# Four small-head attentions: ScalarE's exponentials of a sequence in one run, and a copy moved from ScalarE to VectorE

## The reference, cut to what matters

```python
def heads(x):                       # (8, 128, 128) -> (8, 16, 128, 8)
    return x.reshape(B, S, 16, 8).transpose(0, 2, 1, 3)
qh, kh, vh = heads(q @ wq + bq), heads(k @ wk + bk), heads(v @ wv + bv)
scores = einsum('bhqd,bhkd->bhqk', qh, kh) / sqrt(8)
scores = where(mask, -inf, scores)  # in the first and the last layer only
out = einsum('bhqk,bhkd->bhqd', softmax(scores), vh)
x = x + merge(out) @ wo + bo        # the first layer has an MLP in place of wo
```

## Time and profile before

| | |
|---|---|
| median of 3 runs | 1392.16 us (1392.0 to 1392.6) |
| the profiled execution | 1387.83 us, span 1386.0 us |
| mean granted TensorE clock | 0.896 |
| TensorE matmul busy | 1144.6 us (83%) |
| VectorE busy | 790.0 us (57%) |
| ScalarE busy | 654.6 us (47%) |
| exponentials of the four attentions (line 873) | 128, 69.0 us, mean 598 ns |

### The profile page before, as it was taken

One profiled execution on the slowest core, in us unless ns is written; L12 is line 12 of the kernel. 1 busy time (PEld: TensorE's weight loads), 2 busy tenths in 40 slices (PEclk: granted clock), 3 DMA queues, 4 the chain that ended last, 5 costly groups with the idle time before them and its releaser, 6 DMA issues. The chain is left out here.

```text
span 1386.0 us, 25064 instructions
## 1 busy us (share of the span) xinstructions
PE 1144.6 (83%) x9532; PEld 734.7 (53%) x9532; DVE 790.0 (57%) x1974; ACT 654.6 (47%) x1370; POOL 325.8 (24%) x321
## 2 busy tenths in 40 slices
PE   6998895559798987759877973979889988898998
PEld 4565453337465653327635742847434444465776
DVE  3565446567565458887787878456362565452111
ACT  2564333441253225586687672534666442334332
POOL 1333200013301003754546440140000034300000
PEclk9999998566799997887997996899899998899999
DMA  7000000200000000000000000061095700000000
GB/s 298 1 2 1 1 2 1 90 4 1 0 3 1 0 1 0 0 1 2 1 1 2 2 1 1 2 258 84 17 200 125 153 1 2 1 2 1 1 1 16
DMA packets 15206, 44.39 MB, mean 32 GB/s; under 512 B 1872, under 2 KB 4976, under 8 KB 14448
## 3 DMA queue, kind: packets, MB, share of 16 engines
q1 hardware_dynamic: 15088, 42.80, 10.6%
HBM read 42.01 MB, written 0.79 MB: 31 GB/s over the span
## 5 line engine op out<-in xcount | busy, mean ns | idle before, releaser
L873 ACT ACTIVATE L_xattn_pT<-banks 128x512 f32<-128x512 f32 x128 | 69.0, 598 | 107.2 <-PE banks L757 107.2
L243 POOL TENSOR_TENSOR norm_rstd<-norm_var,norm_power 128x4 f32<-128x4 f32 x24 | 24.6, 1025 | 365.6 <-DVE norm_var L236 365.6
L927 DVE TENSOR_REDUCE L_xattn_top<-banks 128x4 f32<-128x512 f32 x128 | 79.5, 685 | 43.4 <-PE banks L728 43.4
L1511 DVE TENSOR_TENSOR L_ffn_a<-L_ffn_a,L_ffn_share 128x512 f32<-128x512 f32 x64 | 39.9, 687 | 60.2 <-DMA L_ffn_share<-L_ffn_shares 60.0
L1425 PE MATMUL banks<-L_ffn_a,region_a 128*128 128x512 f32 x136 | 67.5, 601 | 5.1 <-DVE L_ffn_a L1511 5.1
L1744 ACT ACTIVATE L_ffn_aT<-banks,L_ffn_shift 128x512 f32<-128x512 f32 x64 | 43.3, 687 | 58.9 <-PE banks L1696 57.3
L1416 PE MATMUL banks<-hT,region_a 128*128 128x512 f32 x136 | 68.9, 612 | 0.0
L1757 DVE SCALAR_TENSOR_TENSOR x<-banks,L_ffn_combine,x 128x128 f32<-128x128 f32 x64 | 18.0, 345 | 88.7 <-PE banks L1707 88.7
L1707 PEld LDWEIGHTS banks<-region_b,L_ffn_aT 128*128 128x128 f32 x512 | 59.4, 192 | 6.7 <-issue 6.7
L492 ACT ACTIVATE L_attn_p<-banks,L_attn_shift 128x129 f32<-128x129 f32 x128 | 45.4, 369 | 35.6 <-DVE L_attn_shift L542 35.6
L1580 PE MATMUL banks<-hT,region_a 128*128 128x512 f32 x128 | 59.4, 608 | 1.3 <-PEq L78 1.3
(11 more groups left out here) (532 smaller groups left out, 2932.1 us busy)
## 6 DMA issues: line engine op xcount, KB each, us to landing
L_ffn_share<-L_ffn_shares SPq DMA_DIRECT2D x32, 512.0 KB, 10.1
region_b<-in_L_ffn SPq DMA_DIRECT2D x1, 6216.0 KB, 29.5
region_a<-in_L_ffn SPq DMA_DIRECT2D x1, 4416.0 KB, 14.1
region_b<-in_L_attn SPq DMA_DIRECT2D x1, 3150.5 KB, 11.6
region_a<-in_L_ffn SPq DMA_DIRECT2D x1, 3080.5 KB, 21.6
region_b<-in_L_attn SPq DMA_DIRECT2D x1, 1633.5 KB, 10.3
region_b<-in_L_xattn SPq DMA_DIRECT2D x1, 835.0 KB, 10.9
w_tables<-in_tables SPq DMA_DIRECT2D x1, 832.0 KB, 13.6
```

The costliest lines, as they stand in the source:

```text
L873: nc.scalar.activation(pT[:, n % 2, 4 * i:4 * i + 4, :], rows_of(flip[i][:], 4), ACT.Exp, scale=scale).then_inc(exped, 1)
L927: nc.vector.tensor_reduce(top[:, 32 * i:32 * i + 32:HD], rows_of(score[i][:], 4), X, ALU.max).then_inc(topped, 1)
L1511: nc.vector.tensor_tensor(a[:, k % AHEAD, :], a[:, k % AHEAD, :], share[:, batch % RING, j, :], ALU.mult).then_inc(weighed, 1)
```

## The change

ScalarE runs the four exponentials of a sequence one after the other and then keep_out; keep_raw leaves it. VectorE does keep_raw(k-2) between find_top(k) and keep_top(k), as a tensor copy. Nothing else is changed: tiles, banks, semaphores and their counts stay.

```diff
@@ ScalarE
-            def keep_raw(n):
-                act.wait_ge(mixed, n + 1)
-                nc.scalar.activation(raw[:], rows_of(mix[:, 0:2 * T], 2), ACT.Copy).then_inc(raw_kept, 1)
-
...
             for k in range(1, LAST):
                 if 0 <= k - 1 < B:
-                    weigh(k - 1, (0, 1))
-                if 0 <= k - 2 < B:
-                    keep_raw(k - 2)
+                    weigh(k - 1, range(G))
                 if 0 <= k - 3 < B:
                     keep_out(k - 3)
-                if 0 <= k - 1 < B:
-                    weigh(k - 1, (2, 3))
                 if carries and k == B + 2:
                     ahead.keep(act, 0, score[2])
@@ VectorE
+            def keep_raw(n):
+                dve.wait_ge(mixed, n + 1)
+                nc.vector.tensor_copy(raw[:], rows_of(mix[:, 0:2 * T], 2)).then_inc(raw_kept, 1)
...
                 if k < B:
                     find_top(k)
+                if 0 <= k - 2 < B:
+                    keep_raw(k - 2)
+                if k < B:
                     keep_top(k)
                 if 0 <= k - 4 < B and out_weight is not None:
                     add(k - 4)
```

## The result

The changed kernel takes 1401.14 us (median of 10 runs, 1397.85 to 1410.73) against 1392.38 us (10 runs, 1386.08 to 1393.8). The ratio on record is 1.0081, 95% interval 1.0057 to 1.0105: slower by 0.8%, where 0.43% was forecast. It is not the quotient of the two medians, which is 1.0063 (+8.8 us); the interval goes with the ratio. The median lies 0.5 us above the range. The profiled execution took 1398.14 us, span 1396.3 us at a mean clock of 0.894; the one of before took 1387.83 us, span 1386.0 us.

The account below looks back on a forecast made before the run. TensorE was taken as the bound. The attentions' terms, +1.72 (first), +1.94 (last) and +1.18 for each unmasked one, made +6.0 us; on the median of 1392.16 that gave 1398.2 us (+0.43%), range 1395.6 to 1400.6.

Parts of the forecast that it names:

- Part 1: Scores of sequences 4 to 7 wait for the later keep_out: +2.20 us a masked attention, +1.44 an unmasked one.
- Part 2: Raw copy on VectorE, 0.40 us long, delays keep_top in step 2: +0.02 us an attention.
- Part 3: Attention ends: flipped scores -0.05 us; last mixing -0.45 us in the first attention, -0.23 in the other three.
- The attentions' sum: All four attentions: first +1.72, last +1.94, the two unmasked +1.18 each, together +6.0 us.
- The early exponentials win: Exponentials and keep_out finish before scores are wanted, only gains left: 1390.2 us; chance 0.03 beyond 0.2%, 0.03 within.
- The delay is partly given back: Scores to E shortens by 0.2 us in each of 16 sequences: 1395.0 us; chance 0.08.
- VectorE becomes the bound: Raw copy of 0.54 us makes keep_top and the norm's work late: +1.3 us, 1399.5 us; chance 0.07.
- The clock falls: Added TensorE idle in the attentions halves its clock for one sequence in each: +12 us, 1410 us; chance 0.03.

Follow-up runs that it names:

- ends alone: Against the kernel before: four exponentials in a row and VectorE's raw copy only in steps 8 and later; 1396.50 us, ratio 1.0050.
- delays: Kernel before, steps untouched, plus useless copies at each attention's end (ScalarE in the first, VectorE in the others), some 6.6 us in all; 1399.67 us, ratio 1.0072.
- keep_out between the pairs: Changed kernel with keep_out put back between the second and third exponential, raw copy still on VectorE; 1393.87 us, ratio 1.0038.
- keep_out alone behind: Kernel before with only keep_out moved behind the last exponential, raw copy still on ScalarE between the pairs; 1402.63 us, ratio 1.0085.
- late wait: Changed kernel with score banks written in the order 0, 2, 3, 1 and the wait for keep_out only before bank 1; 1396.47 us, ratio 1.0060.
- first two attentions: Kernel before with the change only in the attentions of the first two layers, ahead of the delta rule; 1397.61 us, ratio 1.0059.
- last attention: Kernel before with the change only in the last layer's attention, behind which one stage follows; 1393.92 us, ratio 1.0021.
- third attention: Kernel before with the change only in the third layer's attention, which stands behind the delta rule; 1391.67 us, ratio 1.0004.

## Why the prediction was right or wrong

**What bounds the kernel: right.** TensorE does, and ScalarE's freed time brought nothing.

**Part 1, keep_out behind four exponentials: right, with the wait 0.06 us short.** The run of four took 2.06 us as in the earlier trace rows, and keep_out ended at E + 2.23 (177.82 + 0.31 - 175.90) where E + 2.26 was forecast. The scores started not 0.06 us after that but 0.15 (178.28 - 178.13). The forecast took the 0.06 of turn_mixed behind the raw copy. The same rows have 0.15 between keep_out's end (179.44 + 0.28 = 179.72) and the scores (179.87), though nothing shows there that the scores waited for it; with keep_out alone moved back it was 0.14 (178.28 to 178.42). So each masked sequence lost 0.62 us in place of 0.55, and the unmasked period was 5.35 in place of 5.32. From the E of step 3 to that of step 7 the second attention took 21.41 us (21.28 forecast).

**Part 2, the raw copy: right in kind, 0.03 us short at step 2.** It took 0.42 us (0.40 forecast). The E of step 3 came 0.05 us later than before (6.96 in place of 6.91 us after the one of step 2) where 0.02 was forecast. With keep_out out of the way the copy costs 0.04 us a sequence in the unmasked attentions.

**Part 3, the ends: right, but for the flipped scores.** From the last E to the end of the last keep_out the first attention took 5.55 us in place of 5.97, -0.42; the second 5.82 in place of 6.00, -0.18. VectorE's rows of the changed kernel show why the second gained less, as forecast from the earlier trace rows: the raw copy stands right behind the norm's scaling.

```profile
421.38 1.11 DVE L252 TENSOR_SCALAR h<-x,norm_moments,norm_rstd 128x128 f32<-128x128 f32 x4
422.40 0.42 DVE L924 COPY L_xattn_raw<-banks 128x256 f32<-128x256 f32 x1
```

The flipped scores of the last sequence gained nothing: the step from the seventh E to the eighth is 0.03 to 0.05 us longer, not 0.05 shorter.

**The attentions' sum: +6.34 for +6.0, in part by luck.** First +2.13 (1.72 forecast), second +1.48 (1.18), fourth +2.39 (1.94), third +0.34 (1.18). From its step 3 on the third lost as the second did (E of step 3 to that of step 7: 21.41 us in place of 19.85). But in the kernel before it holds a stall of TensorE in step 2, in the middle of one group of matmuls, that none of the three profiles of the changed kernel has:

```profile
941.62 0.85 PE L757 MATMUL banks<-L_xattn_topT,L_xattn_minus 32*128 32x128 f32 x20
943.31 0.71 PE L757 MATMUL banks<-L_xattn_topT,L_xattn_minus 32*128 32x128 f32 x12 [0.83 <-issue]
```

Its cause was not tried. It comes and goes: from the second E to the third this attention takes 5.47 to 6.03 us in the three profiles of the kernel before, 4.90 with the ends alone changed, and 5.99 with the change in this attention alone. Without it the third would have lost what the second did, and the sum would have been near +7.5, 1.5 us over the forecast. That the sum came out near is luck.

**The step that failed** is the one from the sum to the total: that each stage is a block and so nothing later takes the loss up, with about 1 us for where later stages fall on the clock. The median came out 2.9 us over the forecast of 1398.2: 0.2 of it is the median of before (1392.38 for 1392.16), 0.3 the attentions' sum, and 2.4 (4.9 by the ratio, 1.6 to 8.3 by its interval) the stages that the change does not touch. Their time is not a constant to which the attentions' loss is added.

It goes with the time at the half clock. Over the 14 profiled executions, the time outside the attentions was 1197.1 us with 275.5 us of half clock in the fastest (the kernel before), 1200.7 with 289.5, 1204.7 with 297.0 (the changed kernel), 1211.1 with 319.4, and 1215.8 with 326.3 (the delays, 6.6 of it their own). A straight line through the 14 has a slope of 0.33 us for each us of half clock and a correlation of 0.94. The half clock of an execution can be read from its mean clock: (1 - 0.896) x 2 x 1386.0 = 288 us. The unchanged kernel alone shows the same: over its 35 executions of the last session the span goes with the mean clock by a correlation of -0.94, from 1380.5 us at 0.898 to 1396.9 at 0.888. This is a correlation; no run set the clock by itself.

The totals, by the ratio, against what is explained by the attentions (or by the delays' 6.6 us), in us:

| | total over before | explained | beyond, with the ratio's interval |
|---|---|---|---|
| changed kernel | 11.3 | 6.3 | 4.9 (1.6 to 8.3) |
| the same once more | 14.6 | 6.3 | 8.3 (3.8 to 12.7) |
| keep_out between the pairs | 5.3 | 1.0 | 4.3 (2.1 to 6.4) |
| keep_out alone behind | 11.8 | 12.0 | -0.2 (-3.9 to 3.5) |
| late wait | 8.3 | 1.1 | 7.2 (3.9 to 10.4) |
| delays | 10.0 | 6.6 | 3.4 (-0.3 to 7.0) |
| first two attentions | 8.2 | 3.6 | 4.6 (1.5 to 7.8) |
| ends alone | 7.0 | -2.0 | 8.9 (5.7 to 12.1) |
| last attention | 2.9 | 2.4 | 0.5 (-3.5 to 4.6) |
| third attention | 0.6 | 1.4 | -0.8 (-4.5 to 2.8) |

The first eight have something changed ahead of the delta rule. Six of them are clear of zero, the delays just not, and keep_out alone behind the last exponential not at all. The delta rule took 365.9 to 369.0 us in all nine profiles of kernels changed ahead of it, and 361.0, 366.2, 362.7, 362.7 and 367.8 us in the five with nothing changed ahead of it. So a loss beyond the attentions is shown, in most but not all kernels changed ahead of the long stage in which TensorE is busy three quarters of the time, and it goes with time at the half clock. Its cause stays open: why a change there makes the half clock longer on the whole, in either direction of shift, and why it did not for keep_out alone; no run tells whether the kernel before sits on a good alignment of its stages.

**The rivals.** The early exponentials win: refuted, with a gain only at the ends. The delay is partly given back: not seen, scores to E stayed 5.14 us (183.42 - 178.28). VectorE becomes the bound: not in the changed kernel. The clock falls: it had a chance of 0.03 and was looked for in the wrong place. In the attentions it stayed at 1.00, with 0.46 us of idle each masked step; in the delta rule, already in part at the half clock, it went from 0.86 to 0.83 in the first profiles. The Trainium skill, page "TensorE: Matmul & The Clock Gate", says in "What's actually happening" that activity releases the throttle. The trace agrees for the attentions: the two stretches in which TensorE was busy 38.14 of 41 us and 27.42 of 30 us were granted 1.00 throughout.

## What to carry to other kernels

Putting like instructions in a row on an engine that isn't the bound gained nothing in the steady steps here, and what now stood behind the row was late; find for each moved instruction who waits for it and with what work behind. If such a wait guards one bank of several, write that bank last and put the wait there; it took the whole wait away where the banks' first matmuls start one after the other (0.22 us apart in the masked attentions), and only part of it where they start nearly together. In a kernel whose stages run partly at the half clock, an effect of a few us can't be read from the total: compare the touched stage with itself, and take several profiles of both kernels before giving the rest a cause.

## What the runs showed of the hardware

- One unchanged kernel spread over 1382.3 to 1398.7 us in one session, its span going with the mean clock (correlation -0.94 over 35 executions), while the attentions, at full clock, repeat to 0.02 us, the third excepted (40.75 to 41.09 us in three profiles).
- The first matmul came 0.06 us after the end of the copy that it waited for in one place (turn_mixed) and 0.14 to 0.15 us after it in another (the mask and score matmuls behind keep_out).
- Score matmuls of four banks, each on 32 rows of its own, start 0.007 us apart (410.897 to 410.917); full-height 128x512 mask matmuls 0.22 us apart (183.16 to 183.81).
- Four exponentials of 128x512 in a row take 2.06 us (2.06 to 2.07 in every step of the changed kernel), as in the first step of before.
- ScalarE's 128x128 copy took 0.30 to 0.31 us right behind four exponentials, and 0.28 after the raw copy or an idle stretch.
